# Attention maxima: scores of four heads at once over four PSUM banks, masks first

## What is computed

```
q = (x @ Wq.T).reshape(b, s, H, HD)
k = (x @ Wk.T).reshape(b, s, H, HD)
scores = jnp.einsum('bqhd,bkhd->bhqk', q, k) / np.sqrt(HD)
scores = jnp.where(causal, scores, jnp.finfo(scores.dtype).min)
probs = jax.nn.softmax(scores, axis=-1)
```

## Time and profile before

| | |
|---|---|
| median of the runs | 3018.92 us (3018.33 to 3037.64) |
| span of the profiled execution | 2958.7 us |
| TensorE busy | 2351.0 us, 79% |
| VectorE busy | 2163.5 us, 73% |
| ScalarE busy | 1383.5 us, 47% |
| mean granted TensorE clock | 0.870 of 2.4 GHz |

### The profile page before, as it was taken

How to read it: one execution, slowest core, us unless ns; L and a number is a source line. 1 busy time by engine, 2 the same in 40 slices (tenths; PEclk the granted TensorE clock), 3 DMA queues, 4 the chain that set the end, 5 groups by cost and what they waited for, 6 DMA issues and landing times. The chain is left out here.

```text
span 2958.7 us, 36517 instructions
## 1 busy us (share of the span) xinstructions
PE 2351.0 (79%) x12305; PEld 1420.5 (48%) x12305; DVE 2163.5 (73%) x3017; ACT 1383.5 (47%) x2217; POOL 575.3 (19%) x569
## 2 busy tenths in 40 slices
PE   4448896889778977887788869787879688988991
PEld 2335354535453545444544545345535453556880
DVE  4993898489948894899669975998589852246666
ACT  5323654366535663566356634654465424143440
POOL 4000101120131013111311120212120230025661
PEclk8558897899889987998799979998999789988995
DMA  2320231023201321133113311231033182355757
GB/s 105 120 79 8 103 113 57 15 87 128 74 28 60 128 94 35 42 126 107 42 35 109 117 49 42 92 127 56 8 112 121 60 212 97 103 195 174 219 180 302
DMA packets 136229, 292.85 MB, mean 99 GB/s; under 512 B 14288, under 2 KB 79200, under 8 KB 135792
## 3 DMA queue, kind: packets, MB, share of 16 engines
q1 hardware_dynamic: 122224, 251.96, 26.2%
q0 software_dynamic: 13824, 38.55, 3.6%
HBM read 220.91 MB, written 69.54 MB: 98 GB/s over the span
## 5 line engine op out<-in xcount | busy, mean ns | idle before, releaser
L1367 DVE TENSOR_TENSOR_SCAN scan<-scan 128x1024 f32<-128x1024 f32 x256 | 585.9, 2289 | 34.4 <-ACT scan L1097 26.4
L2047 PE MATMUL bank<-ident,scan 128*128 128x128 f32 x2048 | 325.3, 315 | 168.9 <-DVE scan L1376 158.1
L1097 ACT ACTIVATE scan<-scan 128x511 f32<-128x511 f32 x512 | 337.2, 713 | 164.2 <-DVE scan L1367 163.5
L2047 PEld LDWEIGHTS bank<-ident,scan 128*128 128x128 f32 x2048 | 271.6, 162 | 260.1 <-DVE scan L1376 158.4
L1399 DVE TENSOR_TENSOR scan<-scan 128x1024 f32<-128x1024 f32 x256 | 310.5, 1213 | 29.5 <-PE bank L2047 28.5
L1376 DVE TENSOR_TENSOR scan<-scan 128x1024 f32<-128x1024 f32 x256 | 312.0, 1219 | 7.8 <-DVE rest L1579 7.5
L1936 PE MATMUL bank<-hT,wslot 128*128 128x512 f32 x512 | 246.9, 607 | 0.0
L1541 DVE TENSOR_REDUCE rest<-bank 128x2 f32<-128x1024 f32 (+3 forms) x176 | 196.5, 1126 | 66.5 <-PE bank L2118 63.5
L819 POOL DMA_INDIRECT rows_dram<-stage,slot_at x128 | 164.9, 1288 | 370.4 <-DVE scan L1367 313.1
L1144 ACT ACTIVATE rest<-bank 128x2048 f32<-128x2048 f32 (+3 forms) x128 | 158.2, 1236 | 146.7 <-PE bank L2138 146.6
L1936 PE MATMUL bank<-xT,scan 128*128 128x512 f32 (+1 forms) x352 | 185.0, 672 | 7.4 <-ACT xT L983 4.8
(11 more groups left out here) (341 smaller groups left out, 4231.2 us busy)
## 6 DMA issues: line engine op xcount, KB each, us to landing
scan<-bc_dram SPq DMA_DIRECT2D x256, 512.0 KB, 3.8
wslot<-wt SPq DMA_DIRECT2D x64, 384.0 KB, 3.5
rows_dram<-pad SPq DMA_DIRECT2D x32, 670.0 KB
scan<-y_dram SPq DMA_DIRECT2D x32, 512.0 KB, 10.1
rest<-rows_dram SPq DMA_DIRECT2D x108, 134.0 KB, 2.5
scan<-rows_dram SPq DMA_DIRECT2D x52, 134.0 KB, 2.7
scan<-wt SPq DMA_DIRECT2D x4, 1536.0 KB, 13.6
xa<-x SPq DMA_DIRECT2D x8, 512.0 KB, 3.8
```

The source lines that it names most:

```text
L1097: i = a.activation(decay[:, unit % 2, n, 1:], dt[:, c, 1:], ACT.Exp, scale=a_neg[:, c, 2 * pair + n:2 * pair + n + 1])
L1367: d.tensor_tensor_scan(flat, decay[:, unit % 2].rearrange("p n t -> p (n t)"), flat, 0.0, ALU.mult, ALU.add).then_inc(decay_used.sem, 1)
L2047: m = t_.matmul(A.bank(("yT", c))[:, t * P:(t + 1) * P], drive[:, unit % NDRIVE, n, t * P:(t + 1) * P], ident[:, :], is_transpose=True, st ...
```

## The change

The units are put in another order: for each set of head groups half 0 and then half 1, so that unit u-1 and unit u are the two halves of the same heads. The step of an even unit (half 0) writes only its two masks, now with start=True. The step of an odd unit (half 1) writes its two masks and then the scores of all four strips of both units, over four banks, adding to the masks. The reduces of VectorE stay as they are, one for each unit, in the new order. The increment that releases the reduce of the even unit is on the matmul of strip 1 of the last head group, that for the odd unit on strip 3. How the unit steps are woven with other steps is unchanged.

```diff
@@ score_units
         per = SEQ // P // (t + 1)
-        for half in range(2):
-            units += [(t, half, slice(i, i + per)) for i in range(0, NQT, per)]
+        for i in range(0, NQT, per):
+            units += [(t, half, slice(i, i + per)) for half in range(2)]
@@ rest_part of TensorE
-                    width = (t + 1) * P
-                    for i in range(heads.start, heads.stop):
-                        for k in range(2):
-                            rows = slice((2 * half + k) * HW, (2 * half + k + 1) * HW)
-                            at = (i - heads.start) * width
-                            t_.matmul(b[:, k, at:at + width], qT[rows, i, t * P:(t + 1) * P], kT[rows, i, 0:width],
-                                      start=(i == heads.start), stop=False, skip_group_check=True)
-                    n = heads.stop - heads.start
+                    n, width = heads.stop - heads.start, (t + 1) * P
                     for k in range(2):
                         diagonal = b[:, k, 0:n * width].rearrange("p (i k) -> p i k", i=n)[:, :, t * P:]
-                        m = t_.matmul(diagonal, ident_b[:, :], causal[:, :].unsqueeze(1).broadcast_to([P, n, P]), start=False, stop=True, skip_group_check=True)
-                    filled(B, m)
+                        t_.matmul(diagonal, ident_b[:, :], causal[:, :].unsqueeze(1).broadcast_to([P, n, P]), start=True, stop=True)
+                    if half:
+                        pair = [banks(("S", u - 1)), b]
+                        for i in range(heads.start, heads.stop):
+                            for k in range(HPT):
+                                rows = slice(k * HW, (k + 1) * HW)
+                                at = (i - heads.start) * width
+                                m = t_.matmul(pair[k // 2][:, k % 2, at:at + width], qT[rows, i, t * P:(t + 1) * P], kT[rows, i, 0:width],
+                                              start=False, stop=True, skip_group_check=True)
+                                if i == heads.stop - 1 and k % 2:
+                                    filled(B, m)
                     yield
```

## The result

The changed kernel takes 3159.57 us (3152.30 to 3164.93) against 3023.19 for the kernel before beside it: 1.0433 times as long, 95% interval 1.0408 to 1.0457. The forecast was 3057.5, its range 3028 to 3085: slower as forecast, but by 136.4 us and not 38.6, three and a half times as much, and outside the range.

A forecast was written before the change was run, and what follows sets the result against it. Bound taken as a two-deep pipeline of TensorE's scores and VectorE's reduces, TensorE a little behind. Alternation and its followers +30.9 over all turns and ends, clock +7.7, added to median 3018.92: 3057.5 us, range 3028 to 3085.

The forecast's parts named there:

- Four strips cost what two cost: Score matmuls: four strips take 1.13 us at 512 columns, as two do, saving about half of TensorE's 185.4 us.
- The pair cycle: Score stage: two reduces strictly alternating with masks and four-strip scores, 3.80 us a pair at 512 columns against 2.67.
- Rival B: Faster: TensorE's saved time removes VectorE's waits, 2961 to 2990 us, if the step between pairs takes under 0.31; chance 0.06.
- Turn 1 walked through: Score stage of turn 1, unit by unit at nominal clock: last reduce ends 626.3 instead of 623.3, +2.9 us a turn.
- +0.9 behind it: After the last reduce: one dtu step of 0.69 us falls beside POOL's work and costs about 1.64, ahead of line 1550.
- POOL hangs on ACT, not on the reduces: Behind the score stage: POOL would begin within 0.5 us of where it does, though the reduces end later.
- the clock, +7.7 for the whole kernel: Score stage: one pair at 1.2 GHz, 1.1 us more, in each of turns 0 to 6; forecast including it has chance 0.45.
- rival C: Score stage: clock falls early and stays low through the last four pairs, +30.9 + 29, 3079 us; chance 0.12.
- Rival A: Alternation with TensorE staying at 2.4 GHz: +30.9, 3050 us, or 3038 if VectorE's scan chain sets the turn; chance 0.30.
- D: Nothing to see: slack elsewhere swallows the +3, 3019 us; chance 0.07.
- The last turn: +6: Last turn, with filler matmuls and early experts' steps between units: R(21), the last reduce, ends about 6 us later.
- 60.2 us outside the span: Runs' median 3018.92 against profiled span 2958.7: the difference was taken to lie outside the span, unchanged by the edit.

The follow-up runs named there:

- two_strips: Changed kernel, but each unit again writes its own two strips of scores after its own masks: 2965.51 us, ratio 0.9995 to the kernel before.
- pairs_three: Changed kernel with units rotating over three two-bank places, so a pair waits only for the first reduce of the pair before: 3113.91 us, ratio 1.0264.
- filled_waits: Changed kernel with unread matmuls only where its trace showed TensorE waiting for a reduce in the score stage: 3144.85 us, ratio 1.0347.
- all_filled: Changed kernel with unread matmuls both in TensorE's waits of the score stage and in three waits outside it: 3058.54 us, ratio 1.0146.
- one_more: Kernel before with one extra reduce (1.1 us of VectorE a turn) into a scratch row at the last unit: 3115.47 us, ratio 1.0283.
- three_deep: Kernel before with units of scores rotating over three two-bank places, so unit u waits for the reduces of unit u-3: 3062.43 us, ratio 1.0129.
- late_after: Changed kernel with unread matmuls in three TensorE waits outside the score stage: 3088.03 us, ratio 1.0233.
- before_again: Kernel before, unchanged, run and profiled once more on another chip: 3030.97 us, span 3029.2.
- filled_pairs: Changed kernel with five unread matmuls ahead of the masks of every even unit but the first: 3025.19 us, ratio 1.0187.
- three_more: Kernel before with three extra reduces (3.4 us of VectorE a turn) into a scratch row at the last unit: 3010.14 us, ratio 1.0140.
- one_more_late: Kernel before with one extra reduce of 1.13 us a turn and unread matmuls in three waits outside the score stage: 3058.43 us, ratio 1.0119.
- late_before: Kernel before with unread matmuls in three TensorE waits outside the score stage: 3031.09 us, ratio 1.0032.

## Why the prediction was wrong

**Right.** Four strips cost what two cost: 1.14 us at 512 columns, and the scores in all 106.0, of which the low clock has a part, against about half of 185.4. The pair cycle was 3.80 us by the sum and 3.80 to 3.81 by the trace. The mechanism, a two-deep pipeline turned into an alternation, is what two_strips and pairs_three show. Rival B, faster, never came near: the handoff it needed under 0.31 us took 1.45.

**Turn 1 walked through: near, at full clock.** +2.9 us in the stage; 2.0 with the clock held (filled_waits). +0.9 behind it; +1.8 in after and +1.9 in all_filled. Here a step was left out. "POOL hangs on ACT, not on the reduces" holds where the stage kept its clock: in all_filled GpSimd's first tile starts 81.1 us after the turn's first add, 81.0 in the kernel before (86.8 in the changed kernel). But by the walk's own numbers the last reduce ends at 626.3, after GpSimd's start at 624.85, so both quick dtu steps fall beside it, and I counted one. Before, both were over or nearly so when GpSimd started, 1.5 us after the last reduce's end (the second one and GpSimd's start; the first here):

```profile
623.46 0.69 DVE L1343 SCALAR_TENSOR_TENSOR scan<-scan 128x512 f32<-128x512 f32 x1
```

Now it starts at the last reduce's end, and they take 1.60 and 1.64 us instead of 0.69 each:

```profile
634.79 1.27 POOL L843 TENSOR_TENSOR scan<-scan 128x512 f32<-128x512 f32 x1 [22.16 <-ACT scan L1074]
...
635.01 1.60 DVE L1343 SCALAR_TENSOR_TENSOR scan<-scan 128x512 f32<-128x512 f32 x1
...
636.65 1.64 DVE L1345 TENSOR_TENSOR scan<-scan 128x512 f32<-128x512 f32 x1
```

From the last reduce's end to the first add of line 1550 it is 6.7 us instead of 4.9, and from there to the softmax sums 51.2 in both kernels. Together 3.8 was forecast; 2.0 and 1.8 were measured. That the sums agree is luck: one part was 0.9 too large and the other 0.9 too small. Turn 0, which lost no clock later, is +3.6 (309.8 against 306.2, 1.5 and 1.7 of it in and behind the stage) on a forecast of +2.1.

**The term that failed: the clock, +7.7 for the whole kernel.** Measured, it is about 97: 5.1 in the stage and 11.1 outside it in each of turns 1 to 6. Three things were wrong in it.
- *Where it falls.* I looked for it where TensorE idles most, in the last pairs, and charged it there to scores of 1.14 us. It fell at about 599 and 613, after waits between the pairs at 384 columns, and hit the products of lines 1949 and 1936, which are full work: 6.81 us for the first (4.57 before), 2.2 more, then 1.97 + 3.52 for the transposes and products, 2.5 more than before's 1.04 + 1.94. Those two make 4.7 us; filled_waits, where the products of line 1949 are back at 4.62 us, gives 5.1 for the stage, where the forecast has 1.1. I held against rival C that "the two full products between the second and third of these pairs keep TensorE busy"; the full products are what a low clock makes expensive. The Trainium skill, TensorE: Matmul & The Clock Gate, A second HAM failure mode: psum-queue depth-cycling, describes such a case: small idle times while a kernel cycles through PSUM banks make the clock go back and forth, paid between the bursts. The trace agrees, 0.60 and 0.52 where before has 1.00.
- *How far it reaches.* I kept it inside the stage. It cost 11.1 us a turn in two stretches that hold no unit of scores. one_more shows that a delay of 1.1 us does that alone, three_deep that coming 1.0 us early does most of it, late_after that it goes when TensorE gets work in its waits, with the products behind them at full clock again. I had the warning in the rows: the clock was 0.50 at 660, so the kernel before already had falls whose place I left out, and I took for granted that they stay in place when the program shifts.
- *That it repeats.* What turn 1 loses, turns 2 to 6 lost too, to 0.1 us, so an error of a turn is multiplied by six.

Rival A (3050, or 3038), C (3079) and D (3019) fall with it: the first leaves the clock out, C has it in the stage alone, and nothing was swallowed. By terms, for a turn from 1 to 5: alternation and what is late behind it 3.8 (forecast 3.8), clock in the stage 5.1 (1.1), clock outside it 11.1 (0), together 20.0 of 20.5; 0.4 more stands ahead of the first reduce, and its cause wasn't looked for.

**The last turn: +6.** Against before_again it is +10.9, 9.0 of it in the stage of scores (72.3 against 63.4). That stage also holds the unnamed waits in both kernels, so how much of it is the alternation is not settled.

**"60.2 us outside the span".** This was no working but an assumption, and false: 1.8 are outside. It didn't move the forecast, since I added a difference to a median; but a gap of 2% between span and median says that profile and runs come from executions that differ, and the walk should have asked in which part.

**What stays open.** Why a fall of the clock lands on the later stretches for one shift and not for another. Counted from the first reduce to the softmax sums, against the profile before, shifts of -0.9 (three_deep, in the last stretch alone), +1.9 (pairs_three), +2.1 (one_more), +5.4 (filled_waits) and +8.9 (the change) pay there, and 0, +6.5 (filled_pairs) and +6.6 (three_more) do not; the last two ran on another chip than the five, but that chip shows the loss too (filled_pairs has 101.5 and 42.9 in turn 0). A size of the shift that decides it can't be read from this list. The fillers show that the fall can be moved by giving TensorE work, not that I can say where it goes: one_more_late and late_before missed their expectations. And what VectorE waits for in the last turn on some chips.

## What to carry to other kernels

When a change turns TensorE's steady stream into bursts, price the work behind the bursts at half the clock too, not only the bursts: here it was most of the loss in the stage. In a loop whose trace shows falls of the clock at fixed places, a shift of 1 us can cost far more in stages that nobody touched (here 11 us for 1.1 late, 7.5 for 1.0 early), so a small forecast needs that in its range. Before an edit is judged by its time, compare the turn stretch by stretch with the granted clock beside each: a good edit (three_deep) looked bad for that reason alone. Unread matmuls in TensorE's waits tell clock from mechanism, and here they turned that edit into a gain; each set must be measured, since of the five kernels with the later fillers one (late_before) gained nothing and another (one_more_late) lost part of its gain at other places.

## What the runs showed of the hardware

- Work that nobody reads can make a kernel faster: 41 bf16 matmuls in the stage and 44 outside it take the turn from 327.7 to 310.7 us.
- The falls of the granted clock repeat from turn to turn: turns 2 to 5 agree to 0.1 us in two profiles of each kernel. Some runs left the pattern for single turns (all_filled: 321.0 among 310.3 to 310.7; three_more: 317.2 among 314.0 to 314.4); all_filled came back to it.
- The kernel before takes 2966 us on one chip and 3023 to 3037 on others. In the two profiles turns 1 to 5 are equal; 14 us of the difference are in turn 0 and 57 from the last turn on, 16.5 of them VectorE's waits for something unnamed.
